# Attention with relative positions: the probability-times-value sums are issued in runs over three half tiles, and the blocks of a tile's maximum one place earlier

## The reference

```python
attn = einsum('bqc,bkc->bqk', q * scale, k)
attn = attn + rel_h[:, :, :, :, None] + rel_w[:, :, :, None, :]   # by key row, by key column
attn = softmax(attn, axis=-1)                                     # over 2304 keys
out  = attn @ v
x    = x + out @ proj_w + proj_b
```

## Time and profile before

| | |
|---|---|
| median of 3 runs | 6778.15 us (6776.11 to 6785.65) |
| profiled execution, its own time | 6786.55 us |
| its span, first to last instruction | 6784.8 us |
| TensorE busy | 6704.2 us, 99% of the span |
| VectorE busy | 5449.1 us, 80% |
| ScalarE busy | 4750.3 us, 70% |
| GpSimd busy | 939.8 us, 14% |

### The profile page before, as it was taken

How to read it: one execution, slowest core, us unless ns; L and a number is a source line. 1 busy time by engine, 2 the same in 40 slices (tenths; PEclk the granted TensorE clock), 3 DMA queues, 4 the chain that set the end, 5 groups by cost and what they waited for, 6 DMA issues and landing times.

```text
span 6784.8 us, 139135 instructions
## 1 busy us (share of the span) xinstructions
PE 6704.2 (99%) x53504; PEld 4237.1 (62%) x53504; DVE 5449.1 (80%) x9974; ACT 4750.3 (70%) x10225; POOL 939.8 (14%) x967
## 2 busy tenths in 40 slices
PE   7999999999999999999999999999999999999998
PEld 5666666666666666666666666666666666666664
DVE  7887888778887788877888778887888878878883
ACT  3777776767767777677776767767677676767775
POOL 2111010211112110121111211102101121101110
PEclk8999999999999999999999999999999999999999
DMA  6776676767777677667676766767677676777673
GB/s 163 150 157 152 138 160 136 166 151 142 153 147 167 144 145 157 150 156 149 142 153 150 159 144 143 160 146 168 140 145 157 147 165 138 143 152 156 142 155 90
DMA packets 306306, 1013.71 MB, mean 149 GB/s; under 512 B 107440, under 2 KB 196976, under 8 KB 215920
## 3 DMA queue, kind: packets, MB, share of 16 engines
q1 hardware_dynamic: 305648, 1004.81, 69.2%
HBM read 745.26 MB, written 255.69 MB: 148 GB/s over the span
## 4 chain that ended last, share of the span: by engine, by line
PE 95%; DMA 2%; DVE 1%; issue 0%; ACT 0%; POOL 0%; SPq 0%; POOLq 0%; ACTq 0%; DVEq 0%
PE work L807 30%; PE work L880 27%; PE work L798 27%; PE work L826 6%; PE work L845 3%; DMA moving<-rel_scratch 2%; PE work L864 2%; PE work L853 1%; DVE mpart L685 1%; DVE xb L676 0%; ACT probs L562 0%; DMA qk_scratch<-back 0%; DMA back<-attention_scratch 0%; PE work L832 0%; POOL back L506 0%
## 5 line engine op out<-in xcount | busy, mean ns | idle before, releaser
L685 DVE TENSOR_REDUCE mpart<-work 128x1 f32<-128x512 f32 (+1 forms) x8640 | 5078.9, 631 | 1065.1 <-PE work L807 998.7
L562 ACT ACTIVATE probs<-work 128x512 f32<-128x512 f32 (+1 forms) x8640 | 4100.1, 564 | 852.9 <-PE work L798 838.8
L807 PE MATMUL work<-mkeys,hi 128*128 128x512 f32 (+1 forms) x8640 | 3399.1, 394 | 9.4 <-DVE mpart L685 7.2
L798 PE MATMUL work<-moving,keys 113*128 113x512 f32 (+1 forms) x8640 | 3312.8, 384 | 13.5 <-DMA moving<-rel_scratch 7.9
L807 PEld LDWEIGHTS work<-mkeys,hi 128*128 128x128 f32 x8640 | 1644.2, 190 | 606.1 <-DVE mpart L685 322.8
L880 PE MATMUL work<-probs,vall 128*17 128x288 f32 x27648 | 2013.8, 409 | 0.0
L798 PEld LDWEIGHTS work<-moving,keys 113*128 113x128 f32 x8640 | 1641.6, 190 | 396.6 <-ACT probs L562 74.7
L880 PEld LDWEIGHTS work<-probs,vall 128*17 128x17 f32 x27648 | 637.5, 96 | 847.8 <-ACT probs L562 361.8
L826 PEld LDWEIGHTS work<-image,tab 128*48 128x48 f32 x6912 | 401.6, 124 | 545.9 <-ACT probs L562 513.6
L491 POOL TENSOR_TENSOR full<-full,hi 128x384 f32<-128x384 f32 x576 | 584.6, 1018 | 933.2 <-DVE hi L723 933.2
L496 POOL TENSOR_TENSOR rden<-oraw,rden 128x576 f32<-128x576 f32 x96 | 137.2, 1429 | 3946.9 <-DMA rden<-inverse_scratch 3946.9
(11 more groups left out here) (43 smaller groups left out, 629.2 us busy)
## 6 DMA issues: line engine op xcount, KB each, us to landing
moving<-rel_scratch SPq DMA_DIRECT2D x1728, 144.0 KB
moving<-qk_scratch SPq DMA_DIRECT2D x288, 576.0 KB
rel_scratch<-hi SPq DMA_DIRECT2D x192, 432.0 KB, 5.9
rel_scratch<-full SPq DMA_DIRECT2D x192, 432.0 KB, 5.5
moving<-rel_scratch SPq DMA_DIRECT2D x288, 288.0 KB
image<-qk_scratch SPq DMA_DIRECT2D x384, 144.0 KB, 3.2
keys<-qk_scratch SPq DMA_DIRECT2D x192, 288.0 KB, 7.8
qk_scratch<-split_hi SPq DMA_DIRECT2D x144, 192.0 KB, 3.9
```

What stands on the lines that cost most here:

```text
L562: act.activation(probs[:, tile % RING, lo:up], bank[:, 0:up - lo], ACT.Exp).then_inc(act_read, 1)
L685: dve.tensor_reduce(mpart[:, u % 2, q, m:m + 1], bank[:, 0:MSPLIT[m][1] - MSPLIT[m][0]], AX.X, ALU.max)\
L798: pe.matmul(bank[:, 0:up - lo], tile_of(keys[0:K_ROWS, u % 2, :], c, third), moving[0:K_ROWS, slot_of(u, third)[0], lo:up], start=True, st ...
L807: pe.matmul(bank[:, 0:up - lo], hi[:, u % 2, q * P:(q + 1) * P], mkeys[:, u % 2, lo:up], start=True, stop=True).then_inc(for_dve, 1)
```

## The change

Four things change. `probs` holds three tiles instead of two (`RING`), and the space comes from `hi`, which is kept once instead of twice. The sums are issued by half tiles (`attend(tile, part)`), three halves in a row, twice in three tiles: in place 3 of every third tile (`EARLY`), and behind the last score of the tile after it. Max item `m` stands in place `m - 1`, items 0 and 1 both in place 0. The last of the six casts moves from tile 13 to tile 14, and the first one waits for the store of the unit just before, not of the one two before.

```diff
-RING = 2
+RING = 3
+EARLY = 3
...
-                    plan[u][t][m].append(("max", n, q, m))
+                    plan[u][t][max(m - 1, 0)].append(("max", n, q, m))
...
-        hi = sb("hi", [P, 2, N], F32R)
+        hi = sb("hi", [P, N], F32R)
...
-                    if u >= 2:
-                        dve.wait_ge(rel_hi_stored, 32 * (u - 1))
-                dve.tensor_copy(hi[:, u % 2, cols], full[:, cols]).then_inc(hi_ready, 1)
+                    if u >= 1:
+                        dve.wait_ge(rel_hi_stored, 32 * u)
+                dve.tensor_copy(hi[:, cols], full[:, cols]).then_inc(hi_ready, 1)
...
-                        if 8 <= t < 14 and i == 2 and -2 <= u and u + 2 < UNITS:
+                        if 8 <= t < 13 and i == 2 and -2 <= u and u + 2 < UNITS:
                             high(u + 2, t - 8)
+                        if t == 14 and i == 0 and -2 <= u and u + 2 < UNITS:
+                            high(u + 2, NB - 1)
...
-            def attend(tile):
+            def attend(tile, part):
...
-                for part in range(2):
-                    for j in range(4):
...
-                mm.then_inc(attended, 1)
+                for j in range(4):
...
+                if part == 1:
+                    mm.then_inc(attended, 1)
...
-                        if i == SB and 0 < tile <= TILES * UNITS:
-                            attend(tile - 1)
+                        if i == EARLY and t % 3 == 2 and 0 <= u < UNITS:
+                            attend(tile - 2, 0)
+                            attend(tile - 2, 1)
+                            attend(tile - 1, 0)
+                        if i == SB and t % 3 == 0 and 0 < tile <= TILES * UNITS:
+                            attend(tile - 2, 1)
+                            attend(tile - 1, 0)
+                            attend(tile - 1, 1)
```

More of the change, by code:

```diff
@@ L453, in _ @@
                         sp.wait_ge(hi_ready, NB * (u + 3))
-                        rel_store(u + 2, hi[:, (u + 2) % 2, :].bitcast(F32), 0, rel_hi_stored)
+                        rel_store(u + 2, hi[:, :].bitcast(F32), 0, rel_hi_stored)
                     if t == 14 and 0 <= u + 1 < UNITS:
@@ L490, in low @@
                 pool.wait_ge(hi_ready, NB * u + r + 1)
-                pool.tensor_tensor(full[:, cols], full[:, cols], hi[:, u % 2, cols].bitcast(F32), ALU.subtract)\
+                pool.tensor_tensor(full[:, cols], full[:, cols], hi[:, cols].bitcast(F32), ALU.subtract)\
                     .then_inc(lo_ready, 1)
@@ L806, in fill @@
                         pe.wait_ge(mkeys_in[u % 2], 32 * (u // 2 + 1))
-                    pe.matmul(bank[:, 0:up - lo], hi[:, u % 2, q * P:(q + 1) * P], mkeys[:, u % 2, lo:up],
+                    pe.matmul(bank[:, 0:up - lo], hi[:, q * P:(q + 1) * P], mkeys[:, u % 2, lo:up],
                               start=True, stop=True).then_inc(for_dve, 1)
@@ L866, in fill @@
                     mm.then_inc(for_dve, 1)
-            def attend(tile):
+            def attend(tile, part):
                 u, t = divmod(tile, TILES)
                 _, b, h = unit(u)
-                if t == 0:
+                if t == 0 and part == 0:
                     if h == 0:
@@ L876, in attend @@
                 pe.wait_ge(act_read, scored(tile))
-                for part in range(2):
-                    for j in range(4):
-                        at = (2 * j + part) * QCOL
-                        mm = pe.matmul(sums[32 * j:32 * j + VCOL, part, 0:QCOL], vall[:, b * QT + t, h, :],
-                                       probs[:, tile % RING, at:at + QCOL], start=(t == 0), stop=(t == TILES - 1))
-                mm.then_inc(attended, 1)
+                for j in range(4):
+                    at = (2 * j + part) * QCOL
+                    mm = pe.matmul(sums[32 * j:32 * j + VCOL, part, 0:QCOL], vall[:, b * QT + t, h, :],
+                                   probs[:, tile % RING, at:at + QCOL], start=(t == 0), stop=(t == TILES - 1))
+                if part == 1:
+                    mm.then_inc(attended, 1)
             for u in range(-3, UNITS + 2):
```

## The result

| | before | after |
|---|---|---|
| median of 4 runs | 6781.28 us (6776.11 to 6785.65) | 7118.84 us (7114.33 to 7121.34) |
| profiled execution, its own time | 6786.55 us | 7121.34 us |
| its span | 6784.8 us | 7119.6 us |
| granted clock of TensorE, mean | 0.995 | 0.995 |

The ratio is 1.0494, 95% interval 1.0481 to 1.0506: **4.9% slower**, 338 us. The forecast was 279 us, in a range up to 347 above the median that was shown then.

The account below looks back on a forecast made before the run. TensorE's own pace was taken to bound the kernel, with its readers holding three banks each. New waits of 379 us plus 25, less 125 saved by fewer runs, made +279 us: 7057 us, range 6890 to 7125, forecast chance 0.80.

Parts of the forecast that it names:

- The saving of 125 us: Fewer runs of sums, two instead of three per three tiles, were to save 1.30 us a unit, 125 us in all.
- Rel at the seam: Where tiles meet with rel, TensorE waits for ScalarE's banks, at rel and tile 1's last score: 1.90 us a unit.
- Maximum at seams without rel: Where tiles 13/14 and 16/17 meet, TensorE's max blocks wait for VectorE's banks: 1.18 us a unit.
- Casts: Each cast pushes VectorE back 0.26 us; at three seams 0.11 was counted: 0.33 us a unit, between 0 and 0.78.
- First score behind the mid-tile run: The first score after the run in mid-tile waits for its bank, 0.22 us or about 0.05: 0.54 us a unit.
- Sum: Waits of 379 us, plus 25 for extra items, less 125 saved: +279 us, so 7057 us, 4.1% slower.
- Units with extra items: Units with v or fin give VectorE one more reading per tile from tile 12 on: 25 us, between 0 and 50.
- Where it costs nothing: The third `probs` tile, single `hi` and last cast in tile 14 were to cost nothing; SyncE delayed part of a tile.
- the bounds: Weight loads not waiting for banks would give 6923 us, banks free earlier 6913; full casts, v and fin 7125.

Follow-up runs that it names:

- the short pair: The kernels before and after, each with VectorE and ScalarE reading only 64 columns of each score and max bank: 6716.75 us and 6706.75 us.

## Why the prediction was right

It was right in its sign, its mechanism and, within the range, its size: the readers' three banks, not their mean share, decide whether the longer stretches between runs can be filled. Point by point:

- **The saving of 125 us**: 1.30 us a unit; 1.35 in the units of the short pair that don't wait for a row of `moving`, 1.34 in those with qk once the wait for its copy is counted. The total of the pair shows only 10 us of it. The run of 24 matched to 0.01.
- **Rel at the seam**: 1.90 worked out, 3 x 0.31 + 0.91 = 1.84 measured, and with the max behind it, 0.04 late at each of the four seams, 2.00.
- **Maximum at seams without rel**: 1.18 worked out. Tiles 14 and 17 measured 0.63 and 0.59, of which 0.14 in tile 14 (behind mt) was there before: 1.08.
- **Casts**: 0.33 worked out; 0.31 measured, 0.10 to 0.11 in each of tiles 11, 12 and 15.
- **First score behind the mid-tile run**: this term was mis-sized. 0.54 was worked out. In tiles 0 and 3 the first score is 0.22 late, in 6 and 9 0.04; that was to be all, with the block behind it, but the max behind it is 0.075 late besides in all four, the last score 0.09 late in tiles 6 and 9, and the run 0.04 late in 0 and 3 and 0.11 in 6 and 9. That makes 2 x (0.22 + 0.075 + 0.04) + 2 x (0.04 + 0.075 + 0.09 + 0.11) = 1.30, 0.76 more. The prediction followed the late reader to its first victim, and no further.
- **Sum**: 0.76 more here and 0.10 more at rel, 0.10 less at the max and 0.02 less at the casts make 0.74. The run behind the last score of tile 1 was 0.11 late in the kernel before, which the prediction did not count, and there is none in this place now: 0.63 are left, beside the 0.60 (3.25 - 2.65) by which a unit without extra items exceeds the forecast, 58 us over 96 units. The saving was larger by 0.05; the account closes to that.
- **Units with extra items**: 25 us forecast and 25 us measured, but the agreement is partly luck. The term counted VectorE's readings of v and fin; loads also wait 46.0 us for ScalarE's copies of qk, which it didn't count. Units 4 to 6 of a stage, which have qk items, grow by 4.25, 3.71 and 3.70 us (mean of stages 2 to 7), 1.9 us a stage more than three units without extra items. In the seven stages with qk that is about 13 of the 25 us, which leaves v and fin about half of what was forecast for them.
- **Where it costs nothing**: wrong by 0.3% for the late cast, taken alone; it cost SyncE 2 us a unit, where a microsecond and a half was forecast, and fin was late, which the prediction did not think of. In the kernel after fin hardly waits, for a reason that no run here isolates.

On the bounds, the Trainium skill's rule that weight loads are pulled ahead of matmuls in flight ("TensorE: Matmul & The Clock Gate", Part 3, The mechanism) doesn't help a late block here: the load at 4414.41 idled 0.38 us and started with its matmul. The Trainium skill's warning that emptying the banks may become the limit ("TensorEngine Tiling (Array Packing)", PSUM Bottleneck, where it is given for tiled matmuls) fits what this trace shows, with 16% of the chain on the two readers.

## What to carry to other kernels

A run of other work between two stretches of blocks also gives the readers time to empty their banks. Before runs are merged, count for each reader, from the last point where it was idle, how many blocks TensorE issues until it needs a bank again, and compare with start + readings + end; then go on to the next place where the reader has a real gap, because everything up to there can be late as well. One reader made quicker, or given a bank more, only takes away its own part, and the other reader's waits come up: here quicker readers gave 139 and 149 us alone, and 412 together, and a fourth bank gave 106 or 178 us.

## What was not expected of the hardware

- That SyncE's queue has so little to spare: a stand of 2.0 us a unit (189.9 us in 94 cases) came back as 17 us in the two units of a stage with fin, and a stand of 0.8 us (68.5 in 85) as nothing that can be measured.
- That the block behind a late one is late too, whatever it is, though not by one figure. The earlier trace rows had it from a single place, with 0.11. Behind the late second max of tiles 14 and 17 it is 0.10, for the run behind the late last score of tiles 6 and 9 0.11, behind the late first score 0.075, and behind late rel 0.04.
